# An adapter's bias product with 128 rows instead of 2, and another order of work in the tenth unit of each pass

## The chip, the cores and the metric

The kernel runs on one core of a Trainium2 chip. The metric is the device time of one execution in microseconds (us). TensorE (PE in the profile, PEld its weight load) multiplies, VectorE (DVE), ScalarE (ACT) and GpSimd (POOL) do the elementwise work, SyncE (SP) issues DMAs. Each has a queue of its own that it works off in order; they wait for one another on semaphores.

## What is computed

Two rounds of a block and an adapter on 32 sequences of 64 tokens with 512 channels, in float32:

```python
# block (layers 0 and 2): V = 512, H = 2048
attn = softmax(q @ k.T * scale); attn_out = (attn @ v) @ Wp + bp
cms_out = gelu(attn_out @ cW1 + cb1) @ cW2 + cb2 + one_hot(target_codes)
modifier = gelu(concat([attn_out, cms_out]) @ mW1 + mb1) @ mW2 + mb2
x = clip(x + cms_out + modifier, 0, 1)
# adapter (layers 1 and 3), W_down (3, 512, 256), W_up (3, 256, 512), chosen per sequence by its role
h = gelu(x @ W_down[role] + b_down[role])
y = x + h @ W_up[role] + b_up[role]
x = layernorm(y) * gamma[role] + beta[role]
```

## The kernel before, in words

The work goes in four passes: two halves of 16 sequences (1024 tokens), and in each half two layers, where a layer is one block and the adapter behind it. p is the pass, p = 2 * half + layer. Every float32 operand is split in two parts (HI by ACT, LO = value - HI by DVE, line L1408), and a product of two operands is three matmuls (HI HI, HI LO, LO HI), all issued at L664 by the helper `product`.

**The MLPs.** The two MLPs of a block run in 16 units (`UNITS`), u = 0 to 7 for the first and 8 to 15 for the second (`NG` = 8); each makes 256 of the 2048 hidden channels for 1024 tokens and multiplies them down. Units 0 and 8 are plain. The others form the hidden channels by Strassen's scheme, seven products P1 to P7 (`term`, on TensorE in the order P1, P5, P6, P2, P7, P4, P3); in the second MLP a term is 12 matmuls of 512 columns (6 from `aop`, the attention's output, 6 from `cop`, the first MLP's), in the first 6. P7 ends U, from which DVE's `make_z22` makes z22; P3 ends what `make_z12` needs. The hidden quadrants H00, H11, H10, H01 come from ACT's gelu (`hidden`) after P2, z22, P4 and z12. Unit 8's down products are plain too: `down(p, 8, b, ...)` is, for each half b of the tokens, four products of 6 matmuls, one per block of 128 output channels, into four PSUM banks, from which DVE adds them to `acc` (`add`, L1674 for unit 8). Units 9 to 14 (`FAST`) do their down products by Strassen as well: `fast_down(p, u, i)`, with parts of W2 split by ACT's `split_part` and DVE's `low_part`, sums of hidden quadrants by DVE's `hidden_sum` (L1639), split by ACT's `split_sum` and DVE's `low_sum`, and DVE's `fast_add` (L1653) behind each product. GpSimd makes the sums of weights (`combine`, `combine_down`).

TensorE works one unit behind with the down products: while it makes the terms of u it does the down products of u - 1 in between. So the terms of u=9 stand among `down(p, 8, 0)` and `down(p, 8, 1)`, and those of u=10 among fast_down(9, P5), P3, P1, and so on. The order of each engine is written out by hand: on TensorE in `mlps`, on ACT and DVE in `second_unit`, where `then` is true for units whose predecessor is fast (10 to 15) and false for u=9 alone. In u=9 ACT does, after H00: `split_part` P5, `weight_part` (10, P1), H11 (which waits until all down products of unit 8 are through), `split_part` P3, `weight_part` (10, P5), `split_part` P1 and P6, H10, `split_sum` P5, and so on; DVE follows in a like order, with the four adds of `down(p, 8, 1)` behind `low_part` P3. `slot` gives the SBUF places of weights: (10, P5) takes the place of unit 9's P7 and so waits for that term.

**The adapter.** Behind the MLPs come eight tiles (`TILES`) of 128 tokens, i = 0 to 7; each holds two sequences of one role, but the last tile of the second half (passes 2 and 3), which has two roles (`general`). Per tile TensorE does `front` (12 matmuls of 256 columns at L952 and one bias product at L955), `residual` (4 transposes, L965), `turn_h` (2 transposes, L977) and `adapter_up` (6 matmuls of 512 columns at L989 and one bias product at L992); in layer 0 also `turn_back` (4 transposes, L1001). A tile of two roles takes both matmul groups and both bias products twice. The order in iteration i is front(i + 2), turn_h(i + 1), residual(i + 1), turn_back(i - 2), adapter_up(i). DVE does for a tile `clip`, `split_x` (xz, behind ACT's part), `split_h`, `row_stats` and `normalise`; TensorE's front(i) waits for split_x(i). Behind tile 6 stand on ACT and DVE the splits of the first four pieces of the next pass's x (`split_block`, xs).

A bias product multiplies `all_ones` (for a tile of two roles `first_ones` or `last_ones`), slices of the stationary tile `onz`, by a stretch of `brow`, the moving tile. Both have two rows: the HI and LO part of the biases in `brow`, and ones in `onz`. `brow` lies in SBUF over `cop`'s parts for P5 and P6 (a place that P5 and P6 free when unit 15 is through with them) and is loaded once a pass by SP at L530, in SP's queue behind the load of `xp` and ahead of that of `raw_u` (the adapter's up weights, L532). `onz` is filled once, at the start, by GpSimd.

## Time and profile before

| what | us |
|---|---|
| median of 3 executions (lowest, highest) | 2070.95 (2069.89, 2071.57) |
| the profiled execution, its own time | 2071.11 |
| its span, from the first to the last instruction | 2069.2 |

| engine | busy us | share of the span |
|---|---|---|
| TensorE (PE) | 2048.5 | 99% |
| weight loads (PEld) | 1692.9 | 82% |
| VectorE (DVE) | 1513.9 | 73% |
| ScalarE (ACT) | 1020.3 | 49% |
| GpSimd (POOL) | 356.0 | 17% |

The chain of work that ended last is 93% TensorE's, 4% DVE's. How to read it: matmuls overlap, a matmul of 512 columns is recorded with 0.39 us though they start some 0.23 apart, so the busy time of TensorE hides how closely they follow one another, and start times say more. The row "x12" of a timeline is twelve instructions in a run; its us goes from the first start to the last end. Idle time of an engine that nobody waits for costs nothing.

### The profile page before, as it was taken

Reading aid. Unit: us, or ns where it says so; the run is one execution under the profiler, and the core shown is the slowest. Engines: PE = TensorE matmul, PEld = TensorE weight load, DVE = VectorE, ACT = ScalarE, POOL = GpSimd, SP = SyncE. Lnnn points to the kernel's source line nnn. Section 1 sums busy time; section 2 is a strip of 40 time slices with the busy share of each in tenths; the row PEclk is TensorE's granted clock in tenths of the full one; section 3 lists DMA queues with packets and bytes.
Section 4 is the critical chain, followed back from the end, with each engine's and each line's share of the span. In section 5 each row is a group of like instructions: output and inputs, shape, how many; then the busy total and the mean of one; then the engine's idle time right before and its main releaser. Section 6 shows DMA issues by size and latency. Waiting matters only on the chain.

```text
span 2069.2 us, 27672 instructions
## 1 busy us (share of the span) xinstructions
PE 2048.5 (99%) x9500; PEld 1692.9 (82%) x9500; DVE 1513.9 (73%) x2353; ACT 1020.3 (49%) x1844; POOL 356.0 (17%) x378
## 2 busy tenths in 40 slices
PE   8999999999999999999999999999999999999998
PEld 7888887888788888788888888788888888878886
DVE  6576677888767666888877666788876766768877
ACT  5464454555356444555435544555534645445552
POOL 0011112321101102232000110223100111032211
PEclk9999999999999999999999999999999999999999
DMA  7411211212321121112460112022342011111143
GB/s 286 164 31 41 72 46 62 72 62 107 143 82 40 53 73 50 46 62 72 174 209 31 43 60 74 28 72 72 109 157 93 13 59 52 67 61 61 47 142 93
DMA packets 42377, 169.77 MB, mean 82 GB/s; under 512 B 5625, under 2 KB 9721, under 8 KB 34809
## 3 DMA queue, kind: packets, MB, share of 16 engines
q1 hardware_dynamic: 42096, 167.97, 23.4%
q8 instruction: 80, 1.31, 0.3%
q14 instruction: 57, 0.46, 0.1%
q10 hardware_dynamic: 144, 0.03, 0.0%
HBM read 146.97 MB, written 21.01 MB: 81 GB/s over the span
## 4 chain that ended last, share of the span: by engine, by line
PE 93%; DVE 4%; issue 1%; ACT 1%; DMA 0%; SPq 0%; DVEq 0%; ACTq 0%
PE psum L664 83%; PE psum L989 2%; PE psum L952 2%; PE psum L761 1%; PE psum L739 1%; PE psum L992 1%; PE psum L965 1%; DVE acc L1677 0%; DVE fpart L1408 0%; DVE acc L1674 0%; PE psum L977 0%; DVE wdp L1408 0%; PE psum L955 0%; PE psum L762 0%; PE psum L741 0%
## 5 line engine op out<-in xcount | busy, mean ns | idle before, releaser
L664 PE MATMUL psum<-hs,wd 128*128 128x512 f32 x1920 | 448.2, 390 | 0.5
L664 PEld LDWEIGHTS psum<-hs,wd 128*128 128x128 f32 x1920 | 360.2, 188 | 76.7 <-DVE acc L1677 2.2
L664 PE MATMUL psum<-cop,wsm 128*128 128x512 f32 x1416 | 354.8, 389 | 0.0
L664 PE MATMUL psum<-aop,wsm 128*128 128x512 f32 x1320 | 333.2, 390 | 0.0
L664 PE MATMUL psum<-aop,wsc 128*128 128x512 f32 x1320 | 311.4, 390 | 0.0
L664 PEld LDWEIGHTS psum<-cop,wsm 128*128 128x128 f32 x1416 | 265.9, 188 | 55.0
L664 PEld LDWEIGHTS psum<-aop,wsm 128*128 128x128 f32 x1320 | 247.9, 188 | 51.5
L664 PEld LDWEIGHTS psum<-aop,wsc 128*128 128x128 f32 x1320 | 247.6, 188 | 51.3
L1653 DVE TENSOR_TENSOR acc<-psum,acc 128x1024 f32<-128x1024 f32 x144 | 175.8, 1221 | 87.1 <-PE psum L664 86.9
L1677 DVE TENSOR_TENSOR acc<-psum,acc 128x512 f32<-128x512 f32 x256 | 167.6, 685 | 84.2 <-PE psum L664 84.1
L1408 DVE TENSOR_TENSOR hs<-hs_raw,hs 128x512 fp32r<-128x512 f32 x256 | 178.4, 705 | 43.5 <-ACT hs_raw L1229 43.4
L1228 ACT ACTIVATE hs<-psum,bias 128x512 fp32r<-128x512 f32 x120 | 82.1, 684 | 237.2 <-PE psum L664 237.2
L664 PE MATMUL psum<-hs,wdp 128*128 128x512 f32 x576 | 147.4, 392 | 7.7 <-issue 6.2
L1228 ACT ACTIVATE hs<-zt,bias 128x512 fp32r<-128x512 f32 x112 | 81.0, 724 | 128.8 <-PE psum L664 87.6
L664 PEld LDWEIGHTS psum<-hs,wdp 128*128 128x128 f32 x576 | 107.2, 188 | 34.0 <-issue 12.3
L1157 ACT ACTIVATE wsm<-w1m 128x512 fp32r<-128x512 f32 x156 | 96.1, 622 | 38.0 <-DMA w1m<-m_in 38.0
L1408 DVE TENSOR_TENSOR wsm<-w1m,wsm 128x512 fp32r<-128x512 f32 x156 | 110.7, 726 | 0.9 <-ACT wsm L1157 0.9
L664 PE MATMUL psum<-t,wdp 128*128 128x512 f32 x432 | 109.7, 390 | 0.0
L1659 DVE TENSOR_TENSOR zt<-psum,zt 128x512 f32<-128x512 f32 x56 | 38.7, 692 | 80.4 <-PE psum L664 80.4
L664 PEld LDWEIGHTS psum<-t,wdp 128*128 128x128 f32 x432 | 81.1, 188 | 16.8
L606 POOL TENSOR_TENSOR comb<-w1c 128x256 f32<-128x256 f32 x28 | 21.5, 767 | 420.7 <-DMA w1c<-c_in 420.7
L664 PE MATMUL psum<-fw,xs 128*128 128x512 f32 x384 | 93.1, 395 | 0.0
(191 smaller groups left out, 3027.2 us busy)
## 6 DMA issues: line engine op xcount, KB each, us to landing
w1m<-m_in SPq DMA_DIRECT2D x32, 1024.0 KB, 4.9
w1c<-c_in SPq DMA_DIRECT2D x32, 512.0 KB, 3.5
w<-c_in SPq DMA_DIRECT2D x32, 512.0 KB, 3.6
w<-m_in SPq DMA_DIRECT2D x32, 512.0 KB, 3.5
gains<-roles_in SPq DMA_DIRECT2D x30, 512.0 KB, 4.6
fw<-fused SPq DMA_DIRECT2D x6, 2048.0 KB, 10.2
fused<-fw SPq DMA_DIRECT2D x4, 2048.0 KB, 7.5
xmid<-x SPq DMA_DIRECT2D x4, 2048.0 KB, 6.6
```

Of the source, the lines that this page charges most:

```text
L606: nc.gpsimd.tensor_tensor(st, w_block(u, 1, 0), w_block(u, 1, 1), ALU.add).then_inc(w1_sums, 1)
L664: mm = nc.tensor.matmul(out, lhs(a), rhs(b), start=(start and n == 0), stop=(stop and n == total - 1), skip_group_check=reopened)
L739: nc.tensor.matmul(out, tq[:, j // 2, HI, j % 2, i * P:(i + 1) * P], xs[:, :, j, tile], start=(j == 0), stop=False)
L761: nc.tensor.matmul(out, val[:, HI, v_cols], val[:, :, p_cols], start=True, stop=False)
L952: nc.tensor.matmul(out, tokens, wdn_flat[:, bass.ds(role * (2 * KC * BN) + (c * KC + k) * BN, BN)], start=(b == 0 and k == 0 and a == c), ...
L989: nc.tensor.matmul(u_bank[i % 3][:, :], tokens, wup_flat[:, bass.ds(role * (4 * V) + (c * 2 + k) * V, V)], start=False, stop=False)
L1157: nc.scalar.activation(slot(u, i)[:, HI, :], w_source(u, i), ACT.Copy).then_inc(s_hi[i], 1)
L1228: nc.scalar.activation(hs[:, b, HI, m, :], h_source(h, u), ACT.Gelu, bias=b1)
L1408: return nc.vector.tensor_tensor(out, a, hi.bitcast(F32), ALU.subtract)
L1653: nc.vector.tensor_tensor(dst, bank, dst, ALU.add).then_inc(acc_done, 1)
L1659: nc.vector.tensor_tensor(zt[:, 2, :], bank_b()[:, :], zt[:, 2, :], ALU.add).then_inc(z22_done, 1)
L1677: nc.vector.tensor_tensor(dst, d_out[o][:, :], dst, ALU.add).then_inc(acc_done, 1)
```

## The change

`brow` and `onz` get 128 rows. GpSimd zeroes all of `brow` once a pass, behind its sums for the last unit, when P6 of unit 15 is through (the semaphore `brow_zeroed`); SP waits for that instead of for P6 and then loads the two rows of biases. `onz` is zeroed over 128 rows, and ones are written into its first two rows alone. So the 126 further rows of both operands are zero.

In u=9 the order changes on three engines. TensorE does the first two products of `down(p, 8, 1)` ahead of P7 and the other two behind it. ACT does `split_part` P3 and `weight_part` (10, P5) ahead of H11, and `split_part` P1 and P6 behind H10 and `split_sum` P5. DVE does `make_z22` behind `weight_part` (10, P1) and `low_part` P3, and `low_part` P1 and P6 behind `make_z12`.

```diff
-        brow = at("brow", [2, BROW], F32R, CO + 38)
+        brow = at("brow", [P, BROW], F32R, CO + 38)
-        onz = at("onz", [2, 4 * SEQ], F32R, CT + 2.5625)
+        onz = at("onz", [P, 4 * SEQ], F32R, CT + 2.5625)
...
                     if u + 1 == UNITS:
-                        sp.wait_ge(prod[P6], STRASSEN * (p + 1))
+                        sp.wait_ge(brow_zeroed, p + 1)
                         if p == 0:
                             sp.wait_ge(rows_stored, 32 * LAYERS)
-                        sp.dma_start(brow[:, :].bitcast(F32), brows[layer]).then_inc(brow_loaded, 16)
+                        sp.dma_start(brow[0:2, :].bitcast(F32), brows[layer]).then_inc(brow_loaded, 16)
...
             nc.gpsimd.memset(onz[:, :].bitcast(F32), 0.0).then_inc(made, 1)
             pool.wait_ge(made, 11)
-            nc.gpsimd.memset(all_ones.bitcast(F32), 1.0).then_inc(made, 1)
+            nc.gpsimd.memset(onz[0:2, SEQ:3 * SEQ].bitcast(F32), 1.0).then_inc(made, 1)
...
                         if fast(u):
                             combine_down(p, u)
+
+                    pool.wait_ge(prod[P6], STRASSEN * (p + 1))
+                    nc.gpsimd.memset(brow[:, :].bitcast(F32), 0.0).then_inc(brow_zeroed, 1)
...
                         down(p, u - 1, 0)
-                        terms(p, u, P2, P7)
-                        down(p, u - 1, 1)
+                        terms(p, u, P2)
+                        if fast(u):
+                            down(p, u - 1, 1, 0, 1)
+                            terms(p, u, P7)
+                            down(p, u - 1, 1, 2, 3)
+                        else:
+                            terms(p, u, P7)
+                            down(p, u - 1, 1)
                         terms(p, u, P4, P3)
...
                     weight_part(p, u + 1, P1)
-                    hidden(p, layer, u, H11)
-                    split_part(p, u, P3)
-                    weight_part(p, u + 1, P5)
-                    split_part(p, u, P1, P6)
-                    hidden(p, layer, u, H10)
-                    split_sum(p, u, P5)
+                    if then:
+                        hidden(p, layer, u, H11)
+                        split_part(p, u, P3)
+                        weight_part(p, u + 1, P5)
+                        split_part(p, u, P1, P6)
+                        hidden(p, layer, u, H10)
+                        split_sum(p, u, P5)
+                    else:
+                        split_part(p, u, P3)
+                        weight_part(p, u + 1, P5)
+                        hidden(p, layer, u, H11)
+                        hidden(p, layer, u, H10)
+                        split_sum(p, u, P5)
+                        split_part(p, u, P1, P6)
                     weight_part(p, u + 1, P6)
...
                         low_part(p, u, P5)
-                        make_z22(p, u)
                         weight_part(p, u + 1, P1)
                         low_part(p, u, P3)
+                        make_z22(p, u)
                         add(p, layer, u - 1, 1, *range(KC))
                     weight_part(p, u + 1, P5)
                     if then:
                         fast_add(p, u - 1, P2)
-                    low_part(p, u, P1, P6)
+                        low_part(p, u, P1, P6)
...
                     make_z12(p, u)
+                    if not then:
+                        low_part(p, u, P1, P6)
                     weight_part(p, u + 1, P6)
```

## Rows read from the trace of the kernel before

**Rows 1.** The page, first part: busy us, share of the span, instructions.

```profile
PE 2048.5 (99%) x9500; PEld 1692.9 (82%) x9500; DVE 1513.9 (73%) x2353; ACT 1020.3 (49%) x1844; POOL 356.0 (17%) x378
```

**Rows 2.** Waits of TensorE: who waited for whom, us in total, times, longest us.

```profile
PE psum L664 <- issue: 6.2, 4, 1.6
...
PE psum L664 <- DVE acc L1653: 1.5, 4, 0.4
```

**Rows 3.** Timeline, TensorE, u=10 of pass 0: start, us, instruction, [idle before].

```profile
331.44 1.52 PE L664 MATMUL psum<-aop,wsm 128*128 128x512 f32 x6
...
332.80 1.52 PE L664 MATMUL psum<-cop,wsm 128*128 128x512 f32 x6
...
335.88 1.63 PE L664 MATMUL psum<-hs,wdp 128*128 128x512 f32 x6 [1.55 <-issue]
...
344.90 1.62 PE L664 MATMUL psum<-hs,wdp 128*128 128x512 f32 x6 [0.38 <-DVE acc L1653]
```

**Rows 4.** Timeline, VectorE, the same stretch.

```profile
328.29 2.72 DVE L1674 SCALAR_TENSOR_TENSOR acc<-psum,bias,acc 128x512 f32<-128x512 f32 x4
...
332.19 0.69 DVE L1639 TENSOR_TENSOR hs_raw<-t_raw,hs_raw 128x512 f32<-128x512 f32 x1
...
332.98 1.59 DVE L1639 TENSOR_TENSOR zt<-hs_raw 128x512 f32<-128x512 f32 x1
...
335.10 0.68 DVE L1408 TENSOR_TENSOR hs<-hs_raw,hs 128x512 fp32r<-128x512 f32 x1
...
338.82 1.23 DVE L1653 TENSOR_TENSOR acc<-psum,acc 128x1024 f32<-128x1024 f32 x1
```

**Rows 5.** Timeline, ScalarE, the same stretch.

```profile
326.26 0.72 ACT L1228 ACTIVATE hs<-zt,bias 128x512 fp32r<-128x512 f32 x1 [6.13 <-PE psum L664]
...
328.95 0.67 ACT L1229 ACTIVATE t_raw<-psum,bias 128x512 f32<-128x512 f32 x1
```

**Rows 6.** Groups by form, TensorE: xcount | busy us, mean ns | idle before.

```profile
L992 PE MATMUL psum<-brow,onz 2*128 x34 | 16.8, 496 | 0.0
```

**Rows 7.** Timeline, TensorE, adapter of pass 0 (layer 0).

```profile
516.79 1.59 PE L952 MATMUL psum<-wdn,xz 128*128 x12
...
518.11 0.28 PE L952 MATMUL psum<-wdn,xz 128*128 x1
...
518.32 0.38 PE L955 MATMUL psum<-brow,onz 2*128 x1
...
518.62 0.33 PE L965 MATMUL psum<-ident,xct 128*128 128x128 f32 x1
...
526.04 1.70 PE L952 MATMUL psum<-wdn,xz 128*128 x12 [0.30 <-DVE xz L1408]
...
545.60 1.70 PE L952 MATMUL psum<-wdn,xz 128*128 x12
```

**Rows 8.** Timeline, TensorE, adapter of pass 1 (layer 1).

```profile
1027.87 1.70 PE L952 MATMUL psum<-wdn,xz 128*128 x12 [0.30 <-DVE xz L1408]
...
1046.04 1.69 PE L952 MATMUL psum<-wdn,xz 128*128 x12
...
1052.77 0.49 PE L992 MATMUL psum<-brow,onz 2*128 x1
...
1053.19 1.65 PE L989 MATMUL psum<-wup,hz 128*128 x6
```

**Rows 9.** Timeline, VectorE, the same stretch.

```profile
1026.93 0.69 DVE L1408 TENSOR_TENSOR xz<-xct,xz 128x512 fp32r<-128x512 f32 x1 [0.70 <-ACT xz L1358]
...
1043.90 0.69 DVE L1408 TENSOR_TENSOR xz<-xct,xz 128x512 fp32r<-128x512 f32 x1 [0.70 <-ACT xz L1358]
```

**Rows 10.** Memsets of GpSimd's L644; timeline of TensorE and SyncE at unit 15.

```profile
L644 POOL MEMSET xzg<- x2: 527/528/528, 1516.9 to 2022.7; 128x512 f32 x2
...
487.12 0.84 PE L664 MATMUL psum<-cop,wsm 128*128 128x512 f32 x3
...
491.48 0.30 SPq L530 DMA_DIRECT2D brow<-brows  x1
```

More of the change, by code:

```diff
@@ L226, in cond_seq_kernel @@
         ids_loaded, ranked = sem("ids_loaded"), sem("ranked")
-        rows_made, rows_stored, brow_loaded = sem("rows_made"), sem("rows_stored"), sem("brow_loaded")
+        rows_made, rows_stored, brow_loaded, brow_zeroed = (sem(n) for n in ("rows_made", "rows_stored", "brow_loaded", "brow_zeroed"))
         xs_hi, xs_lo = sem("xs_hi"), sem("xs_lo")
```

## Prediction

> **What bounds the kernel now.** The first part of the page: TensorE is busy 2048.5 us of 2069.2 [rows 1]. So there is something to win only where it stands still, or where its instructions lie wider apart than usual. The wait view of TensorE shows how little it stands still: "issue" 6.2 us in four waits, and 1.5 us in four on DVE's L1653, one of each per pass [rows 2]. The timeline puts both into the tenth unit of a pass, u=10, counted from 0 [rows 3]. For the spacing I read the timeline at start times: a bias product of two rows starts late and holds up its successor [rows 7]. There are 34 on L992 [rows 6], and by the code as many on L955. Last I read DVE's timeline beside TensorE's, for what takes over once TensorE is faster.
>
> **Part one, the stall at u=10.** Six matmuls of 512 columns take 1.36 us from start to start (331.44 to 332.80), so a term of the second MLP 2.72. From 332.80 on come the second half of P1 (1.36), fast_down(9, P5) (1.36), P5 (2.72), fast_down P3 (1.36), P6 (2.72), and then fast_down P1, which would start at 342.32. It starts at 344.90: 2.58 us lost [rows 3]. The four passes have the same waits [rows 2], so 10.3 us in all.
>
> Why: fast_down(9, P5) needs low_sum P5, which DVE starts at 335.10. Its queue has hidden_sum P5 at 332.19, and ahead of that the four adds of unit 8 (from 328.29, 2.72 us) and the weight splits [rows 4]. But ACT had H10, the input, at 328.95 + 0.67 = 329.6. DVE is 2.6 us late because ACT held back: H11 waits until unit 8's last plain-down product is through, 6.13 us of idling to 326.26, and the split of P3 is queued behind it on ACT [rows 5], with the adds behind its other half on DVE.
>
> After the change, on TensorE: P3 and P4 of unit 9 stay where they are, so P4 starts at 331.44 - 5.44 = 326.0; half of the down products (2.72) stand before it, and P7 ends at 323.3 to 323.4, 2.72 later than now. On ACT, P3's split and weight part (10, P5) go ahead of H11; the second takes the slot of unit 9's P7, so it comes at 323.5 and ends by 324.2. On DVE z22 follows P7, done by 324.2 (H11 reads it at 326.26, P4 needs its bank at 326.0: 1.8 to spare). The adds follow the down products; the last product ends at 326.2, the last add by 326.9, (10, P5) by 327.5. DVE is idle when H10 comes, and hidden_sum P5 starts at 329.7. low_sum started 2.91 behind it, of which 0.9 is hidden_sum P6 taking 1.59 instead of 0.69 [rows 4] while GpSimd worked on the sum that split (10, P5) releases; that sum now runs in DVE's idle time. So low_sum starts at 331.7 (332.6 if the hold stays) and ends 0.7 later, where TensorE arrives at 334.16. The wait goes, with 0.8 us to spare at worst.
>
> What is late next is fast_down P1, which waits for fast_add P3: DVE needs 6.08 us from fast_add P5 at 338.82 to TensorE's start at 344.90 [rows 3, 4]. fast_add P5 came 3.72 us behind the start of low_sum; now the splits of P1 and P6 stand in between, of half the width of a 0.68 one, 0.35 each. 331.7 + 3.72 + 0.7 + 6.08 = 342.2, against 342.3 wanted. No wait, by a hair; with the 0.9 of the hold it is 0.8 per pass. Behind that DVE and TensorE are both 2.6 us earlier and keep their distance. No DMA is issued in the moved lines; SP's loads wait for parts of unit 9 that are made no later than now. I take 10.3 us, the ends being 7 and 10.3.
>
> **Part two, the bias products.** Twelve products of L952 start 0.12 us apart (516.79 to 518.11). The bias product starts 0.21 after the last, and its successor 0.30 after it: 0.09 + 0.18, with rounding 0.28 us over the spacing [rows 7]. On L992 the successor comes 0.42 later (1052.77 to 1053.19), where a 512-column matmul takes 0.23, so 0.19, and with the same lead-in 0.29 [rows 3, 8]. Every neighbour has 128 rows. With 128 rows in onz and brow the bias product has their form, and I price it at their spacing. The whole is 34 x 0.57 = 19.4 us; the other end is 0, if it is not the rows that break the spacing.
>
> The Trainium skill has it both ways. TensorEngine Tiling, Key Properties, says that a change of the tiling mode drains the engine; by that, all 19.4 us can be had. TensorE: Matmul & The Clock Gate, in the table of its section on why this matters for kernels, gives a single matmul of K=32 the time of one of K=128, which speaks against this change: by that it brings 0. The trace shows time lost around the two-row product and so sides with the first; that the rows are its cause, no row can say.
>
> Not all of it reaches the end, since DVE is nearly as busy in the adapter as TensorE:
> - At front(3) TensorE waits 0.30 us for DVE's xz [rows 7]. That chain starts at the end of the first bias product and goes through ACT's gelu and splits, then DVE's split of wup, three adds, clip and split. It gains the lead-in of 0.09, and 0.10 as that product gets as short as its neighbour (0.38 and 0.28): 0.19 per pass. The other bias products up to here only buy waiting.
> - From front(3) to front(7) are four tiles. In a pass of layer 1 they take 1046.04 - 1027.87 = 18.17 us [rows 8] and would take 4 x 0.57 less, 15.9. But DVE's splits for the same two tiles lie 1043.90 - 1026.93 = 16.97 apart [rows 9], and it idles there only for ACT's round trip. So DVE sets it: 1.20 won, 1.39 with the 0.19. In a pass of layer 0 the transposes back come on top: 545.60 - 526.04 = 19.56, less 2.28 is 17.28, still over 16.97 [rows 7, 9]. All of the 2.28 counts.
> - Behind front(7)'s products follow one L955 and three L992. Pass 0: 0.19 + 2.28 + 0.28 + 0.87 = 3.6, less 0.1 in which TensorE waits for DVE's first piece of the next xs, so 3.5. Pass 2 ends in a tile with two roles and has one more of each: 4.2. Pass 1: 1.39 + 0.28 + 0.29 = 1.96 up to where the next xs hangs on DVE; the later two would give more, but TensorE then waits for xs: 2.05. Pass 3: 1.39 + 0.56 + 0.29 = 2.24, then DVE's last three tiles of statistics set the end, where its last wait of 0.3 goes: 2.5.
> Sum 3.5 + 2.05 + 4.2 + 2.5 = 12.25 us.
>
> The zeroing: GpSimd clears 2304 elements per partition once a pass. 512 take 0.53, so at most 2.4. It waits for P6 of unit 15, through at 487.12 + 0.84 = 488.0, when GpSimd has nothing to do, and ends by 490.5; SP comes to brow's load, behind that of xp, at 491.48 [rows 10]. Hidden, with 1 us to spare; raw_u's load behind it goes out as before. Cost 0, nothing below; no DMA or semaphore is removed. onz's clearing has as many elements per partition as before: 0.
>
> **Sum.** 2071.1 (the profiled execution's own time) - 10.3 - 12.3 = 2048.5. That execution stands 0.16 us over the median, which changes nothing here.
>
> **Rivals.**
> - The row count is not the reason: part one alone, 2060.7. (So the page on the clock gate would have it.) Against it: only these products have two rows, and only they lose. 8%.
> - The later P7 hurts. Slot (10, P5) and z22 come 2.7 us later, and if something in ACT's or DVE's queue hangs on them that I did not follow, low_sum stays late or fast_down P1 waits, up to the whole of part one: 2050.5 to 2058.8. For it: the 0.1 us by which fast_down P1 comes out. 12%.
> - DVE is no limit in the adapter: its idling for ACT shrinks with TensorE's time. Up to 2071.1 - 19.4 - 10.3 = 2041.4. Against it: no TensorE instruction is in that round trip. 6%.
> - Slower: the zeroing comes late. If it takes T, the loads of brow and raw_u go out T - 3.4 late (488.0 to 491.4). If all of that reaches TensorE, four passes eat the 22.6 us from T = 9.1 on; at 12 us it is 2083. Four times what the row of 512 gives. 3%.
> - My forecast, 2046 to 2051.5: 68%; 3% for what I don't see.
>
> The range of 8 in 10 is 2044 to 2057: my case, most of the second rival, the errors of both sums. A measurement of this kernel can tell 0.2% (4 us) from no change; faster by more 0.94, within it 0.03, slower 0.03.
>
> **What would show it.** Part one: fast_down P1 10.9 us behind the start of P1 of u=10, and hidden_sum P5 right behind ACT's H10. Part two: 0.12 and 0.12 around L955, 0.23 around L992; TensorE waits 1.2 us for xz at front(3) in all passes, and 0.5 us twice more in those of layer 1. The zeroing: brow's load 0.5 us behind xp's, as now. Wrong if the spacing stays, if passes of layer 0 wait for xz at later tiles, or if a wait for z22 or for fast_add P3 appears.

## The result, and the profile after

| what | before | after |
|---|---|---|
| median of 4 executions (lowest, highest), us | 2071.04 (2069.89, 2071.57) | 2046.63 (2045.22, 2048.77) |
| the profiled execution, its own time | 2071.11 | 2048.77 |
| its span | 2069.2 | 2046.9 |
| ratio of the times, 95% interval | | 0.9885 (0.9870 to 0.9899) |

The change brings 24.4 us; the forecast was 22.6. In the changed kernel the lines of the code stand lower: the product L664 is L667, the front's products and bias L952 and L955 are L961 and L964, the transposes L965 are L974 and L977 is L986, the way up L989 and L992 are L998 and L1001, DVE's L1408, L1639 and L1653 are L1425, L1656 and L1670. The kernel of an experiment has line numbers of its own.

The page's first part, and the waits of TensorE (who waited for whom, us in total, times, longest us), of the kernel after:

```profile
PE 2026.1 (99%) x9500; PEld 1692.3 (83%) x9500; DVE 1513.8 (74%) x2353; ACT 1019.4 (50%) x1844; POOL 360.6 (18%) x382
...
PE psum L961 <- DVE xz L1425: 6.0, 7, 1.2
PE psum L667 <- DVE fw L1425: 3.1, 1, 3.1
...
PE psum L667 <- DVE xs L1425: 0.6, 1, 0.6
PE psum L961 <- DVE xzg L1425: 0.4, 1, 0.4
PE psum L986 <- DVE hz L1425: 0.4, 1, 0.4
```

The two waits of [rows 2], 7.7 us in eight times, are gone. In the adapter and at its end the waits have grown to 7.4 us, all on DVE: seven on xz, one each on xzg, hz and xs. Before there was one on xz per pass alone (waits of TensorE, before):

```profile
PE psum L952 <- DVE xz L1408: 1.2, 4, 0.3
```

So 6.2 us are new. They tell that TensorE got faster there than DVE can follow.

Where the time went, from the start times of TensorE's instructions in both timelines. The first stretch of a pass goes from its first attention product to fast_down P1 in u=10, the second from the adapter's first front product to the next pass's attention (in pass 3 to the end of the span):

| pass | first stretch, before | after | adapter, before | after | gained | forecast |
|---|---|---|---|---|---|---|
| 0 | 289.45 | 286.90 | 38.89 | 35.08 | 2.55 + 3.81 | 2.58 + 3.5 |
| 1 | 291.04 | 288.41 | 36.59 | 35.17 | 2.63 + 1.42 | 2.58 + 2.05 |
| 2 | 289.57 | 287.00 | 42.84 | 37.73 | 2.57 + 5.11 | 2.58 + 4.2 |
| 3 | 291.03 | 288.33 | 46.71 | 43.79 | 2.70 + 2.92 | 2.58 + 2.5 |
| sum | | | | | 10.45 + 13.26 | 10.3 + 12.25 |

The waits of [rows 2] are 7.7 us and the first stretches gain 10.45. A wait is counted from the recorded end of the product before, 0.16 us behind where the next would have started, and some products around the pauses follow one another at 306 to 357 ns instead of 227 (u=10 of pass 0, before). The start times have all of it.

Between the two, from fast_down P1 to the adapter, 0.33 us more fall away in all. Against that, the first attention of this execution starts at 57.25 us where it was 55.45: a start-up in which TensorE waits for the loads and splits of the fused weights, and whose length differs from execution to execution (53.8 to 57.3 us over the traces of this case; e_queues_order, with the same code up to there, starts at 54.10). So 24.0 us gained behind the start-up, 22.3 in the span; a comparison of single executions carries up to 3.4 us of noise from the start-up, and the stretches above do not.

**Part one in the trace.** Timeline of TensorE, VectorE and ScalarE, u=10 of pass 0, kernel after:

```profile
333.26 1.52 PE L667 MATMUL psum<-aop,wsm 128*128 128x512 f32 x6
...
335.98 1.52 PE L667 MATMUL psum<-hs,wdp 128*128 128x512 f32 x6
...
344.15 1.55 PE L667 MATMUL psum<-hs,wdp 128*128 128x512 f32 x6
...
331.46 0.69 DVE L1656 TENSOR_TENSOR hs_raw<-t_raw,hs_raw 128x512 f32<-128x512 f32 x1 [2.09 <-ACT t_raw L1238]
332.26 0.69 DVE L1656 TENSOR_TENSOR zt<-hs_raw 128x512 f32<-128x512 f32 x1
...
333.47 0.69 DVE L1425 TENSOR_TENSOR hs<-hs_raw,hs 128x512 fp32r<-128x512 f32 x1
...
337.87 1.23 DVE L1670 TENSOR_TENSOR acc<-psum,acc 128x1024 f32<-128x1024 f32 x1
...
325.36 0.63 ACT L1166 ACTIVATE wsm<-comb 128x512 fp32r<-128x512 f32 x1 [2.20 <-PE psum L667]
328.08 0.73 ACT L1237 ACTIVATE hs<-zt,bias 128x512 fp32r<-128x512 f32 x1 [2.09 <-PE psum L667]
...
330.74 0.69 ACT L1238 ACTIVATE t_raw<-psum,bias 128x512 f32<-128x512 f32 x1 [1.32 <-PE psum L667]
```

Read against [rows 3 to 5] with 1.82 us taken off, since P1 of u=10 starts at 333.26 here and at 331.44 there. TensorE goes through without a pause: fast_down P5 (335.98) follows two terms' halves behind 333.26, and fast_down P1 comes 10.89 behind it. ACT's weight part (10, P5) is now ahead of H11 (325.36, then 328.08), and DVE stands idle when ACT's H10 comes: hidden_sum P5 at 331.46, right at its end, low_sum 2.01 behind it instead of 2.91, since the sum behind it (332.26) takes 0.69 instead of 1.59. GpSimd's sum, which before ran beside that one (331.68 to 334.02), now runs in DVE's idle time (329.45 to 330.74), as the prediction has it.

**Part two in the trace.** Timeline of TensorE, adapter of passes 0 and 1, and of GpSimd and SyncE at unit 15, kernel after:

```profile
516.00 1.59 PE L961 MATMUL psum<-wdn,xz 128*128 x12
517.43 0.28 PE L964 MATMUL psum<-brow,onz 128*128 x1
517.55 0.60 PE L974 MATMUL psum<-ident,xct 128*128 128x128 f32 x4
...
524.96 1.69 PE L961 MATMUL psum<-wdn,xz 128*128 x12 [1.15 <-DVE xz L1425]
...
1041.80 0.41 PE L986 MATMUL psum<-ident,hgt 128*128 128x128 f32 x2 [0.40 <-DVE hz L1425]
1046.50 1.86 PE L667 MATMUL psum<-xs,fw 128*128 128x512 f32 x7 [0.62 <-DVE xs L1425]
...
487.20 2.03 POOL L644 MEMSET brow<- 128x2304 f32 x1 [3.17 <-PE psum L667]
...
490.12 0.43 SPq L525 DMA_DIRECT2D xp<-xmid  x1
490.65 0.30 SPq L530 DMA_DIRECT2D brow<-brows  x1
```

The successor of the bias product starts 0.12 us behind it, where [rows 7] had 0.30. The price shows one row below: at front(3) TensorE waits 1.15 us for xz instead of 0.30. The zeroing takes 2.03 us and is through at 489.2, 1.4 us before SP comes to brow's load.

### The profile page after: what moved, and what is told of

The parts are those of the page before. It is cut to its first block, busy times and chain, and to the rows that moved or that the text cites. A ratio compares the mean times of both kernels' runs of the same rounds, so it can differ in the third digit from the quotient of the medians.

```text
span 2046.9 us, 27676 instructions
## 1 busy us (share of the span) xinstructions
PE 2026.1 (99%) x9500; PEld 1692.3 (83%) x9500; DVE 1513.8 (74%) x2353; ACT 1019.4 (50%) x1844; POOL 360.6 (18%) x382
## 4 chain that ended last, share of the span: by engine, by line
PE 94%; DVE 4%; ACT 1%; issue 1%; DMA 0%; SPq 0%; DVEq 0%; ACTq 0%
PE psum L667 88%; PE psum L961 1%; PE psum L998 1%; PE psum L742 1%; PE psum L764 1%; DVE acc L1694 0%; ACT xz L1375 0%; DVE fpart L1425 0%; DVE yt L1897 0%; DVE yt L1901 0%; DVE stats L1880 0%; DMA fraw<-fuse_in 0%; PE psum L765 0%; PE psum L744 0%; SPq L421 0%
## 5 line engine op out<-in xcount | busy, mean ns | idle before, releaser
L667 PE MATMUL psum<-hs,wd 128*128 128x512 f32 x1920 | 448.8, 389 | 0.5
L667 PEld LDWEIGHTS psum<-hs,wd 128*128 128x128 f32 x1920 | 360.0, 188 | 76.9 <-DVE acc L1694 2.2
L667 PE MATMUL psum<-cop,wsm 128*128 128x512 f32 x1416 | 354.7, 389 | 0.0
L667 PE MATMUL psum<-aop,wsm 128*128 128x512 f32 x1320 | 333.0, 389 | 0.0
L667 PEld LDWEIGHTS psum<-cop,wsm 128*128 128x128 f32 x1416 | 265.8, 188 | 55.2
L667 PE MATMUL psum<-aop,wsc 128*128 128x512 f32 x1320 | 311.3, 389 | 0.0
L667 PEld LDWEIGHTS psum<-aop,wsm 128*128 128x128 f32 x1320 | 247.7, 188 | 51.5
L667 PEld LDWEIGHTS psum<-aop,wsc 128*128 128x128 f32 x1320 | 247.4, 188 | 51.4
L1670 DVE TENSOR_TENSOR acc<-psum,acc 128x1024 f32<-128x1024 f32 x144 | 175.7, 1220 | 87.4 <-PE psum L667 87.3
L1425 DVE TENSOR_TENSOR hs<-hs_raw,hs 128x512 fp32r<-128x512 f32 x256 | 178.8, 706 | 43.8 <-ACT hs_raw L1238 43.8
L667 PE MATMUL psum<-hs,wdp 128*128 128x512 f32 x576 | 146.2, 389 | 0.0
L667 PEld LDWEIGHTS psum<-hs,wdp 128*128 128x128 f32 x576 | 108.0, 188 | 22.6
L1425 DVE TENSOR_TENSOR wsm<-w1m,wsm 128x512 fp32r<-128x512 f32 x156 | 110.5, 725 | 1.3 <-ACT wsm L1166 0.9
L667 PE MATMUL psum<-t,wdp 128*128 128x512 f32 x432 | 109.6, 389 | 0.0
L667 PEld LDWEIGHTS psum<-t,wdp 128*128 128x128 f32 x432 | 81.1, 188 | 16.8
L667 PE MATMUL psum<-fw,xs 128*128 128x512 f32 x384 | 93.1, 395 | 0.0
## 6 DMA issues: line engine op xcount, KB each, us to landing
fw<-fused SPq DMA_DIRECT2D x6, 2048.0 KB, 10.8
```

What stands on the lines that cost most here:

```text
L667: mm = nc.tensor.matmul(out, lhs(a), rhs(b), start=(start and n == 0), stop=(stop and n == total - 1), skip_group_check=reopened)
L1425: return nc.vector.tensor_tensor(out, a, hi.bitcast(F32), ALU.subtract)
L1670: nc.vector.tensor_tensor(dst, bank, dst, ALU.add).then_inc(acc_done, 1)
```

## The experiments

Every edit is shown against the changed kernel. e_order_only, e_rows_only, e_interleave, e_cover and e_cover_early were executed four times, the others once; for these the stretches count more than the time.

### The two parts by themselves

e_order_only has the new order of u=9 and two rows:

```diff
-        brow = at("brow", [P, BROW], F32R, CO + 38)
+        brow = at("brow", [2, BROW], F32R, CO + 38)
...
-                        sp.wait_ge(brow_zeroed, p + 1)
+                        sp.wait_ge(prod[P6], STRASSEN * (p + 1))
...
-                    nc.gpsimd.memset(brow[:, :].bitcast(F32), 0.0).then_inc(brow_zeroed, 1)
```

> Only the new order of u=9, bias products with two rows. If the two parts are independent: each pass loses the 2.58 us stall at u=10 and nothing else changes, 2071.0 - 10.4 = 2060.6, with fast_down P1 10.9 us behind the start of P1 of u=10. If the new order needed the other part's time (it comes 22 us earlier in each following pass, but nothing in u=9 is tied to absolute time), the gain would differ from 10.4 by more than 1 us. If the order were worth nothing by itself, 2071.

e_rows_only has the 128 rows and the zeroing, and the old order of u=9 on all three engines:

```diff
-                        terms(p, u, P2)
-                        if fast(u):
-                            down(p, u - 1, 1, 0, 1)
-                            terms(p, u, P7)
-                            down(p, u - 1, 1, 2, 3)
...
+                        terms(p, u, P2, P7)
+                        down(p, u - 1, 1)
```

> Only the 128 rows and the zeroing, u=9 in its old order. By the trace of the changed kernel the four adapters are 3.8, 1.4, 5.1 and 2.9 us shorter, 13.3 in all, so 2071.0 - 13.3 = 2057.7, with the old stall of 1.55 and 0.38 us at u=10 in every pass. By my blind sum it would be 12.3, 2058.7. If the row count were not the cause, 2071.

Order only: 2061.36 us (2060.3 to 2062.05), 0.9949 of before (0.9932 to 0.9965). The first stretch has the values of after (286.87 to 288.45), the adapters those of before (38.88, 36.57, 42.83). Rows only: 2056.66 us (2056.12 to 2058.22), 0.9929 (0.9912 to 0.9945); it is the other way round, 289.48 to 291.01 and 35.06, 35.07, 37.71. The product of the two ratios is 0.9878, that of both together 0.9885: the parts add up, neither gives the other anything.

### Whether it is the rows, and how many

e_rows32, e_rows64 and e_rows100 are the changed kernel with another number of rows in both operands:

```diff
-        brow = at("brow", [P, BROW], F32R, CO + 38)
+        brow = at("brow", [32, BROW], F32R, CO + 38)
...
-        onz = at("onz", [P, 4 * SEQ], F32R, CT + 2.5625)
+        onz = at("onz", [32, 4 * SEQ], F32R, CT + 2.5625)
```

> The changed kernel with 32 rows in place of 128. Theory A, the array works in row groups, and any product that does not use all of them breaks the spacing: 0.21 us before and 0.31 behind L964 as with two rows, and about 2060.6. Theory B, only a nearly empty product loses (two rows are a special case): spacing 0.12 and 0.12, about 2046.6. Theory C, the loss falls in proportion to the rows: about three quarters of the loss remain, 0.19 and 0.26, about 2057.

> The changed kernel with 100 rows in place of 128. Theory A, row groups of 32: 100 rows touch all four groups, so the spacing is that of 128, 0.12 and 0.12 round L964, about 2046.6. Theory D, any row count other than the neighbours' 128 breaks the spacing: 0.21 and 0.31, about 2060.6. Theory C, in proportion: a quarter of the loss or less, 0.14 and 0.16.

> The changed kernel with 64 rows in brow and onz instead of 128. 32 rows kept the spacing of two rows (209 and 308 ns around L964, 425 at L1001), 100 rows had that of 128 (117 and 120, 230). Theory A (a stationary of at most 64 rows is laid out in the array otherwise than one of more, so only from more than 64 rows on the product has its neighbours' form): spacing as with 32 rows, adapters 38.9, 36.6, 42.8, 40.6 us, 2059.3. Theory B (only up to 32 rows are laid out otherwise): spacing as with 128, 2046.6. Theory C (the loss falls with the rows): spacing between, near 160 and 210 ns, about 2053.

Medians from start times: from the last neighbour to the bias product, from it to its successor, from that to the next. For the front's, the 28 that turn_h's transposes follow; for the way up's, the two whose successor is a product of 512 columns that waits for nobody. Where a product of 256 columns follows the way up's without a wait, the difference is the same: 327 + 421 + 222 ns before, 226 + 236 + 116 in e_cover, 392 less.

| rows | front's bias, ns | way up's bias, ns | adapters of passes 0, 1, 2 | time, us |
|---|---|---|---|---|
| 2 (before) | 209, 308, 165 | 327, 425, 336 | 38.89, 36.59, 42.84 | 2071.04 |
| 32 | 209, 308, 165 | 326, 426, 336 | 38.88, 36.57, 42.83 | 2059.26 |
| 64 | 209, 310, 168 | 327, 428, 336 | 38.88, 36.70, 42.80 | 2061.12 |
| 100 | 117, 122, 113 | 232, 235, 235 | 35.06, 35.06, 37.78 | 2046.0 |
| 128 (after) | 117, 120, 109 | 232, 231, 235 | 35.08, 35.17, 37.73 | 2046.63 |

There are two cases and nothing between: up to 64 rows a product breaks the spacing of its 128-row neighbours, with 100 it does not. The weight loads show where it is lost. Timeline of the weight loads and of TensorE around a bias product, with 32 rows and then after:

```profile
514.53 0.18 PEld L964 LDWEIGHTS psum<-brow,onz 32*128 32x128 f32 x1
514.84 0.42 PEld L974 LDWEIGHTS psum<-ident,xct 128*128 128x128 f32 x4
...
514.53 0.38 PE L964 MATMUL psum<-brow,onz 32*128 x1
514.84 0.66 PE L974 MATMUL psum<-ident,xct 128*128 128x128 f32 x4
```

```profile
517.31 0.19 PEld L964 LDWEIGHTS psum<-brow,onz 128*128 128x128 f32 x1
517.45 0.46 PEld L974 LDWEIGHTS psum<-ident,xct 128*128 128x128 f32 x4
...
517.43 0.28 PE L964 MATMUL psum<-brow,onz 128*128 x1
517.55 0.60 PE L974 MATMUL psum<-ident,xct 128*128 128x128 f32 x4
```

With 128 rows the loads start 0.12 and 0.10 us ahead of their products, beside the products that still run. With 32 rows load and product are recorded with the same start, for the bias product and for the first of the transposes behind it: nothing is loaded ahead across the border between the two forms, on either side. The successor's successor comes late too (165 for 109, 336 for 235 ns); its load starts 0.06 us behind the late product (514.90) where after the two start together (517.55), which fits, but no run tries this step by itself.

### Which engine's order does it

e_queues_order takes TensorE's new order back and keeps those of ACT and DVE; e_tensor_order does the opposite:

```diff
-                        terms(p, u, P2)
-                        if fast(u):
-                            down(p, u - 1, 1, 0, 1)
...
+                        terms(p, u, P2, P7)
+                        down(p, u - 1, 1)
```

> The changed kernel with TensorE's order of u=9 as before (P7 ahead of all four down products), the new orders of ACT and DVE kept. Theory A, the stall came from ACT's and DVE's queues alone: the last down product of unit 8 still ends when it did, so the last add ends 0.7 us later as now, and fast_down P1 stays 10.9 us behind the start of P1: about 2046.6. Theory B, DVE needs the two down products ahead of P7 to spread its four adds: low_sum P5 comes late again, by up to 2.6 us per pass, up to 2057.

```diff
+                        hidden(p, layer, u, H11)
                         split_part(p, u, P3)
                         weight_part(p, u + 1, P5)
-                        hidden(p, layer, u, H11)
...
+                        make_z22(p, u)
                         weight_part(p, u + 1, P1)
                         low_part(p, u, P3)
-                        make_z22(p, u)
```

> The changed kernel with the orders of ACT and DVE in u=9 as before, TensorE's new order kept. Theory A: nothing of the stall goes, since ACT still holds P3's split behind H11: 13.5 us from P1 to fast_down P1, about 2057. If z22 then comes late as well, a little more. Theory B, TensorE's order is what matters: 10.9 us, about 2046.6.

Queues only: 2045.77 us, first stretch 286.89, 288.42, 287.00, 288.33, as after. TensorE only: 2058.51 us, 289.47, 291.00, 289.58, 290.91, as before, and the waits of [rows 2] are back (waits of TensorE, e_tensor_order):

```profile
PE psum L667 <- issue: 6.2, 4, 1.6
...
PE psum L667 <- DVE acc L1670: 1.4, 4, 0.4
```

All of part one is ACT's and DVE's order. Moving P7 behind two of the down products on TensorE does nothing: DVE is idle ahead of hidden_sum P5 for 2.10 us with P7 in its old place and for 2.09 us in its new one. ACT's order without DVE's, or the other way round, was not tried.

### What limits the adapter now

e_no_bias leaves the 68 bias products out, so the price of a bias product is zero:

```diff
-                    ones = (first_ones, last_ones)[b] if general(half, i) else all_ones
-                    mm = nc.tensor.matmul(out, ones, brow[:, bass.ds(role * BN, BN)], start=False, stop=(b == len(r) - 1))
```

> The changed kernel without the 34 + 34 bias products (the biases of both adapters are left out of the result), so TensorE has 0.12 + 0.23 us less to do per tile. If DVE sets the pace from front(3) to front(7), these four tiles still take 17.0 us in all passes, and what is won is only behind front(7) in layer 0: 1 to 2 us in all, about 2045. If TensorE set it, 34 x 0.35 = 11.9 us less, about 2035.

2045.5 us. The four adapters (35.56, 35.00, 36.45 and 43.21) are together 1.5 us shorter than the changed kernel's (1 to 2 expected; that of pass 2 by 1.3, that of pass 0 is 0.5 longer), though 34 x 0.117 + 34 x 0.231 = 11.8 us of TensorE's work are gone. Its wait for xz grows (waits of TensorE, e_no_bias):

```profile
PE psum L961 <- DVE xz L1421: 9.2, 12, 1.4
```

From front(3) to front(7) it takes 16.92 us in every pass, layer 0 or 1, and after takes 16.93 to 17.01. That is DVE's pace: its splits of the same two tiles lie 16.97 apart in [rows 9] and 16.92 after (1019.35 and 1036.27 in its timeline).

e_interleave fills DVE's idling of 0.70 us per tile, in which it waits for ACT's part of xz, with the first half of the normalisation:

```diff
                         nc.vector.scalar_tensor_tensor(out=y[i % 4], in0=u_bank[i % 3][:, :], scalar=mv[:, s, 0:1], in1=scale[:, 0:V],
                                                        op0=ALU.subtract, op1=ALU.mult).then_inc(yn_done, 1)
+                        if between is not None:
+                            split_x(between)
```

> The changed kernel with DVE's split_x(i + 3) moved between the two halves of normalise(i - 1), so that DVE no longer idles 0.7 us per tile for ACT's part of the split. If DVE's queue is the limit of the adapter in layer 1: its period falls from 4.59 to about 3.9 us, TensorE's waits at front(6), front(7), turn_h(7) and for xs go, some 2.3 us in each pass of layer 1 and up to 0.5 in one of layer 0: 2046.6 - 5 = 2041.5. If the loads of the gains (4.7 us to land, asked for only when the tile two before is through) are next, DVE waits for them and the gain is under 2 us, about 2045.

2045.26 us (2044.31 to 2046.01), 0.9875 (0.9859 to 0.9892): 1.4 us under the changed kernel, which is no more than the times tell apart, and the time of the second theory. The adapters (34.83, 34.61, 37.81 and 42.05) are 2.5 us shorter in all, most of it in pass 3. The idling went and came back as another wait, because the split now stands behind the wait for the gains (waits of DVE, this kernel, and then after):

```profile
DVE yt L1897 <- DMA gains<-roles_in: 5.4, 5, 1.4
```

```profile
DVE yt L1897 <- DMA gains<-roles_in: 0.7, 1, 0.7
```

Only in pass 3, where the gains came in time, front(3) to front(7) fell to 15.32; in pass 1 it is 16.45, in passes 0 and 2 a little over the 16.9 of the changed kernel (17.02 and 17.10).

e_cover covers the same idling with the statistics instead, and leaves the split ahead of that wait:

```diff
+                        if i + 3 < TILES:
+                            if i + 3 == TPB:
+                                dve.wait_ge(acc_done, acc_at(p + 1, 0))
+                            clip(i + 3)
                         if i >= 1:
                             row_stats(i - 1)
                         if i + 3 < TILES:
-                            if i + 3 == TPB:
-                                dve.wait_ge(acc_done, acc_at(p + 1, 0))
-                            clip(i + 3)
                             split_x(i + 3)
```

> The changed kernel, with DVE's clip(i+3) moved ahead of row_stats(i-1), so that ACT's part of xz is made while DVE does the statistics; split_x(i+3) stays ahead of normalise(i-1) and so ahead of the wait for the gains. Theory (DVE's idling of 0.70 us per tile for ACT is what holds the adapter of a layer-1 pass at 4 x 4.59 us per DVE tile after the bias products have become cheap; a later arrival of the gains is then no longer in front of the split): front(3) to front(7) falls from 16.97 to about 15.3 us in both passes of layer 1 (15.32 is what the interleaved version reached in the last pass, where its gains came in time), the passes of layer 0 stay at their 17.0, which TensorE's own work fills; 2046.6 - 2 x 1.65 = about 2043.3. Rival (the gains loads pace DVE wherever the split stands): front(3) to front(7) in pass 1 stays above 16.3 us and the time at 2045, as in the interleaved version. Rival (no effect, DVE is not the limit): 2046.6.

e_cover_early has this, and in addition clip(3) and split_x(3) ahead of the last unit's adds:

```diff
-                    add(p, layer, last, 1, 1, 2, 3)
+                    clip(3)
+                    add(p, layer, last, 1, 1, 2)
+                    split_x(3)
+                    add(p, layer, last, 1, 3)
```

> As the kernel before this one, and clip(3) stands ahead of the adds of blocks 1 to 3 of the last unit, split_x(3) behind two of them. Theory (TensorE's wait of 1.15 us at front(3), in every pass, comes from DVE's three adds, clip and split in a row): DVE starts clip(3) 1.9 us earlier, split_x(3) ends 1.2 us earlier, TensorE does not wait at front(3) (its wait for xz of 6.0 us in seven times falls under 1), front(3) comes at 7.8 instead of 8.97 us from the adapter's start; four passes give 4.6, so 2043.3 - 4.6 = about 2038.7. Rival (what stands behind paces the adapter: DVE's work up to split_x(7) is the same in sum and the gains loads are no earlier): front(3) comes earlier and front(7) does not, the time stays within 1 us of the kernel before this one.

e_cover: 2042.99 us (2042.4 to 2044.3), 0.9865 (0.9849 to 0.9882). The adapters (34.48, 34.60, 37.40 and 42.05) are 3.2 us shorter than the changed kernel's. Front(3) to front(7) is 16.68 in passes 0 and 2, where 17.0 was expected to stay, 15.58 in pass 1 and 15.31 in pass 3. Against e_interleave the adapters gain only 0.8 us; of the 3.3 us between the two profiled executions 2.5 are start-up (54.12 against 56.59). e_cover_early: 2039.69 us (2038.81 to 2039.97), 0.9847 (0.9831 to 0.9864), 3.3 us less again where 4.6 were expected, and 31.7 us below the kernel before in the same series (2071.39), the fastest version here. Front(3) comes at 7.63 to 7.71 us instead of 8.96, in all passes, and TensorE has no wait for xz left. Three adapters get shorter by 0.88, 1.19 and 1.35 us; that of pass 1 gets longer by 0.13. Timeline of VectorE and of TensorE there, and the sum of the waits for gains:

```profile
1026.90 0.75 DVE L1897 SCALAR_TENSOR_TENSOR yt<-psum,mv,gains 128x512 f32<-128x512 f32 x1 [2.72 <-DMA gains<-roles_in]
...
1028.36 0.42 DVE L1425 TENSOR_TENSOR hz<-psum,hz 128x256 fp32r<-128x256 f32 x1
...
1028.92 0.41 PE L986 MATMUL psum<-ident,hgt 128*128 128x128 f32 x2 [1.80 <-DVE hz L1425]
...
DVE yt L1897 <- DMA gains<-roles_in: 8.1, 6, 2.7
```

DVE waits 2.72 us for the gains of a tile, split_h stands behind it in DVE's queue, and TensorE's transposes wait for that. Each step that makes the adapter faster brings its gains nearer: DVE's wait for them is 0.7 us in all after the change, 4.6 in e_cover, 8.1 in e_cover_early. Why they land late in pass 1 (their place in SP's queue, or the load on the DMA engines) was not tried.

### The zeroing made seven times as long

```diff
-                        sp.wait_ge(brow_zeroed, p + 1)
+                        sp.wait_ge(brow_zeroed, 7 * (p + 1))
...
+                    for n in range(7):
+                        if n:
+                            pool.wait_ge(brow_zeroed, 7 * p + n)
+                        nc.gpsimd.memset(brow[:, :].bitcast(F32), 0.0).then_inc(brow_zeroed, 1)
```

> The changed kernel with brow cleared seven times in a row before its load is let go; one clearing takes 2.03 us in the trace, so the seven end about 14.3 us behind P6's end, near 501.6 us in pass 0 instead of 489.2. SP's loads of brow, raw_u and the gains go out at 501.7 instead of 490.7. Theory (chain: raw_u takes 8.5 us to land, ACT's split of it stands ahead of the last hidden quadrant H01, at 501.93 and 506.94 us; the split waits until 510.5 and H01 comes about 5 to 6 us late; the down product behind it waits, the rest is hidden): 20 to 24 us over four passes, 2067 to 2071. Rival (the forecast's pricing of the zeroing, with every us of delay beyond 9.1 reaching TensorE, T = 14.3: 4 x (14.3 - 9.1) = 21): 2067. Rival (all of the 11 us of delay reaches the end): 2090. Rival (hidden, since the adapter needs brow first at 517.4): 2046.6. Told apart by the waits of TensorE, and by what ACT waits for at the first split of the up weights: DMA raw_u or nothing.

The first rival there carries the wrong price: T = 9.1 was where the delay eats the whole gain, and the prediction's own formula was 4 x (T - 3.4). At T = 14.55 that is 44.6 us of delay, on the forecast's 2048.5 a time of 2093, much the same as "all of the delay reaches the end". Measured: 2076.7 us. From fast_down P1 to the adapter a pass takes 178.63 to 178.99 instead of 171.8, 6.8 to 7.2 us more, 27.9 in all, where 20 to 24 were expected; the rest is as after. Timelines of GpSimd, SyncE, ScalarE and TensorE, then two stretches of the same trace (length, busy us of PE, PEld, DVE, ACT and POOL with counts, granted TensorE clock, DMA share, GB/s):

```profile
486.79 14.55 POOL L647 MEMSET brow<- 128x2304 f32 x7 [3.18 <-PE psum L670]
...
501.71 0.36 SPq L532 DMA_DIRECT2D raw_u<-up_in  x1
...
508.18 1.06 ACT L1281 ACTIVATE wup<-raw_u 128x1024 fp32r<-128x1024 f32 x1 [6.55 <-DMA raw_u<-up_in]
511.13 0.72 ACT L1240 ACTIVATE hs<-zt,bias 128x512 fp32r<-128x512 f32 x1 [1.89 <-DVE zt L1684]
...
514.57 7.98 PE L670 MATMUL psum<-hs,wd 128*128 128x512 f32 x24 [4.73 <-DVE acc L1697]
...
504.00:509.00 5.00, 5.00 (x23) 4.13 (x22) 0.75 (x1) 0.82 (x1) 0.00 (x0) 1.00 0.98 388
...
514.50:518.50 4.00, 3.93 (x9) 3.17 (x10) 3.89 (x8) 1.58 (x2) 0.00 (x0) 0.50 0.01 4
```

The chain is the one expected: against the kernel after, whose start-up is 0.4 us longer, SP lets raw_u go 10.8 us later (501.71 for 491.25), ACT's split of it (in its queue ahead of H01) waits 6.55 us, H01 comes 4.6 us later (511.13 for 506.94), and TensorE stands still for 4.73 us. But the loss is 6.9 and not 4.7: the 24 products behind that pause take 7.82 us to the adapter's start instead of 5.62 (510.38 to 516.00), since the granted clock is 0.50 in the stretch behind it, the lower of its two levels, 1.2 GHz, where it was 1.00 before. Ten of these products follow one another at 421 to 427 ns, the later ones at 226 to 233 again. 2.2 of the 6.9 us are the clock's.

## Why the prediction was right, point by point

- **Part one, 10.3 us: held, 10.45.** Its marks came out: fast_down P1 10.89 behind the start of P1 (forecast 10.9), hidden_sum P5 at the end of H10, low_sum at 331.7 + 1.8 = 333.5 (333.47), no 0.9 us of hold. From low_sum to fast_add P5 it is 4.40 (3.72 + 0.7 forecast). fast_down P1, which on paper had 0.1 us to spare, came without a wait. The rival that the later P7 hurts has its condition fulfilled and no effect; e_queues_order adds that P7's place is of no matter at all, which the prediction, in walking through TensorE's order first, did not say. The gain comes from ACT's and DVE's new order; the prediction puts it on ACT's, and the runs do not part the two.
- **The rows are the cause: held,** by the table of five row counts; the rival that they are not falls. The Trainium skill, TensorEngine Tiling (Array Packing), sections Tiling Modes and Key Properties, has row tiles of 128, 64 and 32 rows and says that changing the mode drains the engine; the runs agree with a border above 64 (64 loses, 100 does not), and give the price that it leaves out; whether what happens there is a drain, no run shows. The Trainium skill, TensorE: Matmul & The Clock Gate, section Why this matters for your kernels, gives a single matmul of K=32 the time of one of K=128. Between 128-row neighbours no run agrees: the product with 32 rows costs as much more as that with two, and the measurement decides.
- **The term 0.28 + 0.29 per pair: too small, the one step that was mis-sized.** It went from the last neighbour to the successor, and stopped there. The successor's successor is late as well. For the front's bias (209 + 308 + 165) - (117 + 120 + 109) = 336 ns; for the way up's (327 + 425 + 336) - (232 + 231 + 235) = 390 ns. A pair is worth 0.73 us, all 34 of them 24.7 us and not 19.4. e_cover, where DVE no longer holds up most tiles, bears this out: 19.56 - 4 x 0.726 = 16.66 in layer 0 (16.68 measured), 18.17 - 2.90 = 15.27 in layer 1 (15.31 in pass 3).
- **DVE sets the pace from front(3) to front(7) in layer 1: held,** 16.93 to 17.01 for 16.97, shown by e_no_bias and, from the other side, by e_cover. The rival that DVE is no limit falls: without any bias product the time is 2045.5, not 2041.4. For layer 0 the step said that TensorE stays the slower with 17.28; with the true term its 16.66 is under DVE's 16.97, so DVE limits there too. It takes 16.9 where 17.28 was forecast, which is why 2.60 were won for 2.28. A wait for xz at a later tile of layer 0 was one of the prediction's signs of being wrong, and it came, though a small one: at front(7) of passes 0 and 2 TensorE starts 418 and 415 ns behind the bias product where 234 would do, a wait of 0.18 us that is too small for the wait view.
- **The waits at front(3): held,** 1.15 for 1.2 us, one per pass; front(3) itself comes 0.27 us earlier, 0.19 forecast. The chain that was forecast gains its 0.19 (counted from the adapter's start, ACT's gelu starts at 1.75 us for 1.94). The further 0.08 come from a wait that it left out: before, DVE's split of hz(0) started at 5.05 us, just behind ACT's part of hz, which was ready at 5.02 and hangs on the second bias product; now that part is ready at 4.39, and the split starts at 4.78, as soon as the split of wup lets it. The further waits of layer 1 came at 0.44 and 0.45 in pass 1 and at 0.45 and 0.43 in pass 3 (0.5 forecast).
- **Behind front(7): one too low, one too high.** In pass 2 the stretch gives 14.04 - 11.84 = 2.20 us for 1.73, the larger term again. In pass 1 it gives nothing (9.18 and 9.20) where 0.66 were forecast: turn_h(7) waits 0.40 us for hz, a wait that the prediction did not list, and xs 0.62. So pass 1 falls short by 0.63 us while the adapters' sum is 13.26 for 12.25.
- **The zeroing at no cost: held,** 2.03 us for at most 2.4, brow's load 0.53 us behind xp's as forecast. Its rival had the right chain and an upper bound as a price: at T = 14.55 the loss is 28 us and not 44.6, as some 6 us of raw_u's lateness per pass (10.8 against 4.7 of standstill) are hidden, and the clock adds 2.2.

The two errors of size, the term and layer 0's limit, partly met in DVE's pace: of the 5.3 us by which all bias products were undervalued only 1.0 reached the end. Where a second engine is near, an error in the first one's price is cut off; where it isn't, as in e_cover, the full price is paid out.

## What to carry to other kernels

Give a small product among full ones the same number of rows as its neighbours, with zeros, if the zeroing is done by an idle engine: here 0.34 us for one of 256 columns and 0.39 for one of 512. Price such a product by the spacing of four instructions in a row, until it is the usual one again, and not by its own record. Where one engine waits for the other's instruction in the middle of a queue, look at what is queued ahead of that instruction for no reason, and in which order two waits stand: filling the same 0.70 us of idling per tile brought front(3) to front(7) of pass 1 from 17.01 to 16.45 us where the split came to stand behind a wait for a load, and to 15.58 where it stayed ahead of it. And compare such versions by stretches: their adapters differ by 0.8 us, their times by 2.3.

## What the runs showed of the hardware

- A product of 2, 32 or 64 rows between such of 128: its weights are not loaded ahead and neither are its successor's; 0.34 and 0.39 us each. With 100 rows there is no loss. Where between 64 and 100 the border lies was not tried.
- In e_zero7 4.7 us of a waiting TensorE put the granted clock from 1.00 to 0.50 for the products behind, which cost another 2.2 us. Behind the pause of 1.55 us in [rows 3] it was 1.00 in every stretch of the trace of before (334 to 348 us).
- GpSimd clears 128 x 2304 elements in 2.03 us, 0.9 ns per element of a partition, where [rows 10] had 528 ns for 512; over 32 partitions (e_rows32) it is 2.02 us. DVE's 512-element operations beside it take their usual 0.68 us (487.24 to 489.65 in the timeline after).
- The first attention starts at 53.8 to 57.3 us over these traces, though the code of the start-up is the same but for the rows of onz. The granted clock between 30 and 40 us goes with it: 1.00 in the six traces that start at 53.8 to 54.6, 0.83 in the five at 55.5 to 56.6, 0.66 in the three at 56.9 to 57.3. Behind the start-up, stretches whose code is the same agree within 0.1 us per pass; only the adapter of pass 1 spreads more, 35.06 to 35.45 us with 100 or 128 rows.
